# VectorE with one SBUF operand per instruction in the gather passes, and attention ends in seven groups

## What is computed

```python
x = _layernorm(x + _L0_gnn_ref(x, src, dst, ...))       # norm-weighted neighbour sum, 2 dense layers, gelu
x = _layernorm(x + _L1_gnn_ref(x, ..., src, dst, type)) # attention, 1 head, 8 relations
x = _layernorm(x + _L2_gnn_ref(x, src, dst, ...))       # neighbour sum, 2 dense layers, relu
x = _layernorm(x + _L3_gnn_ref(x, edge_attr, src, dst, ...)) # attention, 4 heads, edge scores
# an attention: logits of each edge, softmax over the edges of a destination, weighted sum
ex = jnp.exp(logits - seg_max[dst]); denom = segment_sum(ex, dst); out = segment_sum(ex / denom[dst] * z[src], dst)
```

## Time and profile before

| | |
|---|---|
| three timed runs, median (lowest, highest) | 10099.64 us (10096.38, 10099.9) |
| the profiled execution | 10036.1 us |
| its span | 10034.4 us |
| busy in the span: POOL, VectorE, ScalarE, TensorE | 7578.5, 3383.1, 1391.9, 493.3 us |
| the 16 DMA engines, mean share by the software queue and the hardware queue | 12.9%, 8.6% |

### The profile page before, as it was taken

The page is one execution under the profiler, slowest core; times in us unless marked ns, Lnnn a source line. Parts: engine busy times, 40 slices in busy tenths (PEclk is TensorE's granted clock), DMA queues, the critical chain, the costliest instruction groups (busy, mean ns, idle before and its releaser), DMA issues. The chain is left out here.

```text
span 10034.4 us, 21314 instructions
## 1 busy us (share of the span) xinstructions
PE 493.3 (5%) x3908; PEld 414.0 (4%) x3908; DVE 3383.1 (34%) x2929; ACT 1391.9 (14%) x1369; POOL 7578.5 (76%) x6764
## 2 busy tenths in 40 slices
PE   6000000000300000000000000000020000000000
PEld 6000000000200000000000000000020000000000
DVE  7222222222432222222225666666323222222222
ACT  0111111111211111111111111111111111111111
POOL 0777777777677777777767777777767777777776
PEclk9999999999655555555555555555555555555555
DMA  1211111111322121221222222222222212122221
GB/s 58 57 47 44 47 47 47 47 47 46 96 50 47 44 47 44 47 47 44 48 57 72 77 78 79 79 79 79 53 34 69 52 48 52 48 52 48 51 51 43
DMA packets 319095, 553.49 MB, mean 55 GB/s; under 512 B 157061, under 2 KB 164980, under 8 KB 311988
## 3 DMA queue, kind: packets, MB, share of 16 engines
q0 software_dynamic: 216064, 226.41, 12.9%
q1 hardware_dynamic: 102942, 326.10, 8.6%
HBM read 298.89 MB, written 253.15 MB: 55 GB/s over the span
## 5 line engine op out<-in xcount | busy, mean ns | idle before, releaser
L445 POOL DMA_INDIRECT rows_a<-table,idx_c_a x3224 | 3750.7, 1163 | 982.5 <-issue 982.5
L445 POOL DMA_INDIRECT rows_l<-table,idx_c_l x3224 | 3519.3, 1092 | 1229.3 <-issue 981.9
L862 DVE TENSOR_TENSOR score_a<-rows_a,target_a 128x26 f32<-128x26 f32 (+1 forms) x124 | 34.2, 276 | 3317.0 <-DMA rows_a<-table,idx_c_a 3317.0
L650 DVE COPY msg_l<-rows_l 128x1664 f32<-128x1664 f32 x124 | 197.2, 1591 | 2721.2 <-DMA rows_l<-table,idx_c_l 2721.2
L797 ACT COPY back_a<-msg_a 128x1690 f32<-128x1690 f32 (+1 forms) x124 | 416.7, 3361 | 516.0 <-DVE msg_a L902 516.0
L545 ACT COPY back_l<-msg_l 128x1664 f32<-128x1664 f32 x124 | 384.6, 3102 | 701.3 <-DVE msg_l L658 701.3
L787 ACT ACTIVATE diff_a<-diff_a 128x52 f32<-128x52 f32 (+1 forms) x124 | 38.6, 311 | 3171.0 <-DVE diff_a L879 3171.0
L436 ACT COPY idx_c_l<-src_i 128x26 int32<-128x26 int32 x124 | 25.8, 213 | 3263.0 <-DVE msg_l L650 3238.9
L902 DVE TENSOR_TENSOR_SCAN msg_a<-keeps_a,msg_a 128x1690 f32<-128x1690 f32 (+1 forms) x124 | 466.3, 3760 | 24.9 <-DVE msg_a L897 24.8
L658 DVE TENSOR_TENSOR_SCAN msg_l<-keeps_l,msg_l 128x1664 f32<-128x1664 bf16 x124 | 451.9, 3644 | 4.5
L419 DVE TENSOR_REDUCE part<-prod_e 125x132 f32<-125x8448 f32 x50 | 447.6, 8953 | 1.7
(11 more groups left out here) (228 smaller groups left out, 1721.3 us busy)
## 6 DMA issues: line engine op xcount, KB each, us to landing
prefix<-back_l SPq DMA_DIRECT2D x124, 832.0 KB, 3.6
prefix<-back_a SPq DMA_DIRECT2D x62, 936.0 KB, 3.7
prefix<-back_a SPq DMA_DIRECT2D x62, 858.0 KB, 3.5
rows_l<-table,idx_c_l POOLq DMA_INDIRECT x3224, 2.5
rows_a<-table,idx_c_a POOLq DMA_INDIRECT x3224, 2.5
feat<-edge_attr SPq DMA_DIRECT2D x50, 1031.2 KB
table<-stage SPq DMA_DIRECT2D x49, 260.0 KB, 2.1
spread<-zero SPq DMA_DIRECT2D x12, 806.0 KB
```

The lines of the kernel that those rows point to most:

```text
L445: pool.indirect_dma_start(rows[:, s * CH + k, 0:row], None, table, bass.IndirectOffsetOnAxis(idx_c[:, s, k:k + 1], 0))\
L650: nc.vector.tensor_copy(msg[:, u], rows[:, s * CH:(s + 1) * CH, :].rearrange("p k f -> p f k")).then_inc(taken, 1)
```

## The change

Inside the four passes every VectorE instruction has at most one operand that lies in SBUF; what it reads beside that lies in PSUM.

- `keeps` becomes one PSUM tile instead of two SBUF tiles. `msg` gets a column ahead of the 26 places; the last column of the chunk before is copied there by ScalarE (semaphore `carried`), and the scan runs over 27 columns. The steps L654, L894 and L897 are gone, and `same0` and `hold` with them.
- In `gather_sum` ScalarE instead of VectorE copies `rows` into `msg`; the order of ScalarE's work changes with it. The parts of the one-hots' comparison come from PSUM, per chunk, put there by ScalarE (`halve`), where two whole rows in bf16 were in SBUF.
- In `attend` scores, running maxima, differences and probabilities lie in two PSUM banks (`work_ps`, `prob_ps`). ScalarE copies the fetched scores in, and takes the exponential in two instructions. The curve of layer 3 takes two instructions where it took one. The running maximum gets a copy in SBUF (`best`).
- The end of an attention works in seven groups of seven blocks, each as soon as its rows land; the squares are VectorE's, the roots ScalarE's, and each group is stored by itself.

```diff
-                msg = tsb(f"msg_{tag}", [P, 2, D, CH])
-                keeps = tsb(f"keeps_{tag}", [P, 2, D, CH], BF16)
+                msg = tsb(f"msg_{tag}", [P, 2, D, 1 + CH])
+                keeps = tps(f"keeps_{tag}", [P, D, 1 + CH])
...
                         for c in range(CHUNKS):
-                            u = c % 2
+                            s, u = c % SLOTS, c % 2
+                            if c:
+                                act.wait_ge(scanned, c)
+                            nc.scalar.copy(keeps[:, :, 1:1 + CH], same16[:, c * CH:(c + 1) * CH].unsqueeze(1).broadcast_to([P, D, CH]))\
+                                .then_inc(keeps_ready, 1)
+                            if c:
+                                nc.scalar.copy(msg[:, u, :, 0:1], msg[:, 1 - u, :, CH:1 + CH]).then_inc(carried, 1)
+                                keep_back(c - 1)
+                            if first and c + HSLOTS < CHUNKS:
+                                act.wait_ge(hot_ready, 2 * (c + 1))
+                                halve(c + HSLOTS)
+                            act.wait_ge(gathered[s], 16 * CH * (c // SLOTS + 1))
+                            if c >= 2:
+                                act.wait_ge(back_ready, c - 1)
+                            nc.scalar.copy(msg[:, u, :, 1:1 + CH], rows[:, s * CH:(s + 1) * CH, :].rearrange("p k f -> p f k")).then_inc(taken, 1)
                             if c + SLOTS < CHUNKS:
                                 lists(act, idx_c, src_i, taken, chunk_ready, c + SLOTS)
...
                             if first and c + HSLOTS < CHUNKS:
                                 dve.wait_ge(counted, c + 1)
-                                one_hots(c + HSLOTS, hot_ready)
-                            dve.wait_ge(gathered[s], 16 * CH * (c // SLOTS + 1))
-                            if c >= 2:
-                                dve.wait_ge(back_ready, c - 1)
-                            nc.vector.tensor_copy(msg[:, u], rows[:, s * CH:(s + 1) * CH, :].rearrange("p k f -> p f k")).then_inc(taken, 1)
+                                hots(c + HSLOTS)
+                            dve.wait_ge(keeps_ready, c + 1)
...
-                            nc.vector.tensor_tensor_scan(flat, keeps[:, u].rearrange("p f k -> p (f k)"), flat, 0.0, ALU.mult, ALU.add)\
+                            nc.vector.tensor_tensor_scan(flat, keeps[:].rearrange("p f k -> p (f k)"), flat, 0.0, ALU.mult, ALU.add)\
                                 .then_inc(scanned, 1)
```

In `attend`, ScalarE's and VectorE's loops:

```diff
                         for c in range(CHUNKS):
...
+                            if c:
+                                keep_back(c - 1)
+                                nc.scalar.copy(msg[:, u, :, 0:1], msg[:, 1 - u, :, CH:1 + CH]).then_inc(carried, 1)
+                                act.wait_ge(diff_ready, c)
+                            act.wait_ge(gathered[s], 16 * CH * (c // SLOTS + 1))
+                            nc.scalar.copy(score, rows[:, s * CH:(s + 1) * CH, score_at:score_at + heads].rearrange("p k h -> p h k")).then_inc(score_in, 1)
                             act.wait_ge(diff_ready, c + 1)
-                            nc.scalar.activation(diff[:, u], diff[:, u], ACT.Exp).then_inc(exp_ready, 1)
+                            nc.scalar.activation(prob, diff[:, 0:heads], ACT.Exp).then_inc(exp_ready, 1)
+                            nc.scalar.activation(fall[:], diff[:, heads:2 * heads], ACT.Exp).then_inc(exp_ready, 1)
...
-                            dve.wait_ge(gathered[s], 16 * CH * (c // SLOTS + 1))
-                            link(nc.vector.tensor_tensor(score[:], fetched[:, :, score_at:score_at + heads].rearrange("p k h -> p h k"), target[:, :, here], ALU.add))
+                            dve.wait_ge(score_in, c + 1)
+                            link(nc.vector.tensor_tensor(score, score, target[:, :, here], ALU.add))
...
+                            for h in range(heads):
+                                last = nc.vector.tensor_tensor_scan(best_ps[:, h, 1:1 + CH], mneg16[:, here], score[:, h], best_ps[:, h, 0:1], ALU.add, ALU.max)
+                                chain.on(last)
...
+                            link(nc.vector.tensor_copy(best[:, u], best_ps))
+                            link(nc.vector.tensor_tensor(diff[:, heads:2 * heads], best[:, u, :, 0:CH], best_ps[:, :, 1:1 + CH], ALU.subtract))
...
-                                link(nc.vector.tensor_tensor(by_head(hold[:]), by_head(msg[:, 1 - u, :, CH - 1]),
-                                                             diff[:, u, heads:2 * heads, 0:1].broadcast_to([P, heads, part]), ALU.mult))
-                                dve.wait_ge(taken, c + 1)
-                                link(nc.vector.tensor_tensor(msg[:, u, :, 0], msg[:, u, :, 0], hold[:], ALU.add))
...
+                        centre(0)
+                        for g in range(1, NG):
+                            centre(g)
+                            finish(g - 1)
+                        finish(NG - 1)
```

257 lines of the change are left out of this document (131 added, 126 removed).

## The result

| | median us | runs | ratio to before |
|---|---|---|---|
| before | 10099.77 | 4 (10096.38 to 10103.22) | |
| changed | 9962.54 | 4 (9960.60 to 9966.73) | 0.9865 (95%: 0.9848 to 0.9882) |

The change gains 137 us where 1170 were forecast; 9962.54 lies 953 us above the range. The execution shown took 9966.73 us, its span 9965.0.

A forecast was written before the change was run, and what follows sets the result against it. POOL's gathers were taken to bound the kernel, held by VectorE reading two SBUF operands or the two-way copy. 10034.4 - 1155 + 4 - 17 + 3 = 8869 us of span, carried to 8930 us timed; range 8850 to 9010.

The forecast's parts named there:

- What bounds the kernel, and what holds a gather: All four passes: POOL's gathers bound; two SBUF reads by VectorE or the two-way copy hold them; 1155 us removable.
- Rival 1: Chunk scans: a scan holds gathers even with `keeps` in PSUM; 715 us of the 1155, 9645 us; chance 0.06.
- Rival 3: Gather passes: only the two-way copy is cured, 169 us and 10 us of ends; 9920 us; chance 0.02.
- Rival 4: All passes: a busy VectorE holds gathers wherever operands lie, only the ends gain; 10090 us; chance 0.01.
- The one-hots: Pass l0: reading PSUM costs VectorE about 134 us and the end nothing, as long as gathers bound.
- The ends: Ends of both attentions: 15.4 us after the last landing become 6.8; -17 us in all, between -10 and -22.
- The sum: Whole kernel: 10034.4 - 1155 + 4 - 17 + 3 = 8869 us of span.
- The step that failed: Span to timed median: the 63.5 us between profiled execution and timed runs was carried over, giving 8930 us.
- Nothing reaches POOL: Chunk loop: VectorE's added work, 8.7 us in l0 and 21.6 in l2, stays under POOL's 32.5 us per chunk.
- the means of 0.944 to 0.96 us a gather: All passes, profile after: gathers nearly bare, 6448 of them some 6115 us busy.
- My own last sentence: All gathers: forecast wrong if the bare gather exceeds 0.944 us with the faster stream, or run-end gathers 1.1 us.
- Rival 2: Chunk loop through PSUM becomes the bound, up to about 10980 us; sign: POOL waits for an index copy; chance 0.03.

The follow-up runs named there:

- fast group: Batches of runs in which the kernel before takes 10037 to 10052 us.
- e1_vector_waits: Changed kernel, but in all four passes VectorE waits for landed gathers and tells ScalarE by a tiny memset; 8853.74 us (0.8813).
- e2_hots_from_sbuf: Changed kernel, but operands of the l0 one-hots lie in SBUF as bf16 again, without ScalarE's copies per chunk; 8915.32 us (0.8875).
- e8_before_again: The kernel before, unedited, run and traced again beside the changed kernel; 10104.87 us.
- e9_vector_waits_2: The text of e1_vector_waits, unedited, run again beside the changed kernel and the kernel before; 9899.09 us.
- slow group: Batches of runs in which the kernel before takes 10076 to 10148 us.
- i2_keeps_in_sbuf_l: Changed kernel, but `keeps` lies in SBUF as bf16 again in gather passes l0 and l2; 9728.04 us.
- j1_keeps_in_sbuf_all: Changed kernel, but `keeps` lies in SBUF in all four passes, bf16 in gather passes, f32 in attentions; 9785.91 us (0.9666).

## Why the prediction was wrong

- **What bounds the kernel, and what holds a gather.** Right, as far as the fast group goes. Beside scans (3.98 us) and multiplies (3.34 us) gathers are bare in e1_vector_waits, and the passes together take 8073 us against 9234 of before in the fast group: 1161 us less, where 1155 were summed. The sentence of the Trainium skill that was weighed there ("SBUF — State Buffer", "Who interferes with whom", the inferred one) is not borne out here: the multiply of two SBUF tiles held a gather for 3.45 us, and with one operand in PSUM the gather beside it takes 0.94. Rivals 1, 3 and 4 fall by the bare gathers beside multiply and scan.
- **The one-hots.** Right that reading PSUM costs VectorE (3621 ns instead of 1878) and that POOL gains: with SBUF operands (e2_hots_from_sbuf) 62 gathers of l0 are held beside a one-hot and the pass takes 2082 us, with PSUM ones (e1_vector_waits, whose wait differs as well) it takes 2019.
- **The ends.** Right: in the changed kernel 6.4 us pass from the last landing to the last product, for 15.4 (forecast 6.8):

```profile
9954.77 0.19 DVE L973 TENSOR_SCALAR rows_a<-agg 128x28 f32<-128x28 f32 x1 [3.73 <-DMA agg<-prefix,endrow]
...
9960.59 0.62 DVE L991 TENSOR_TENSOR xcur<-rows_a 128x448 f32<-128x448 f32 x1
```

- **The sum.** 8869 us of span were forecast. In the fast group e1_vector_waits has 8852.2. The unedited changed kernel was never timed there. An estimate is the 8912.0 of e2_hots_from_sbuf less the 63 us that its l0 is longer than in e1_vector_waits, about 8849. So the sum was right, within some 20 us, for a condition in which the kernel was not timed.
- **The step that failed** is "The median of the timed runs lies 63.5 us above the profiled execution. Carried over as a fixed part it gives 8934, as a ratio 8927, not at all 8871." Half a per cent between a profile and its timed runs, where those agree among themselves within 7 us, was a sign that they were of two conditions (in the batch of e8_before_again, all of it slow, the profiled execution took 10107.93 us and the median of its runs is 10104.87), and the slow one has no fixed price. It costs the kernel before 72 us (10034.4 to 10106.2) and the text of e1_vector_waits 1055 (8852.2 to 9907.3 in e9_vector_waits_2): 915 in the passes, 140 around them. For the changed kernel itself the estimate is 9965.0 - 8849, some 1116. With it fell "Nothing reaches POOL" (16 waits in l0, 367 us) and the means of 0.944 to 0.96 us a gather (992 and 1052 ns). My own last sentence named this case ("if the bare gather itself came out longer than 0.944 with the faster stream"), and gave it no chance. Rival 2's sign, POOL waiting for an index copy, is there in l0, but PSUM traffic and the loop's own work do not bring it by themselves: nearly the same loop (e1_vector_waits) takes 2019 us in the fast group.
- **Where the gain went**, within the slow group (10106.2 to 9965.0, 141 us): a1 -130, l2 -7, a3 -154, l0 +118, l0 to a1 +32, l2 to a3 +8, the tail -8. The attentions had held gathers enough to lose down to 2226 us; l2 had not, and l0 lost. That the time falls at all was forecast for the right reason; that it falls by 137 us is what the slow group left of it.

**Open.** What makes a batch fast or slow, and what in the chip, or in the recording, sets 1.38 us a gather and multiples of 0.7 us on TensorE. Each timed run here carries its own span and granted clock, so it was recorded in some way as well. Semaphore events are missing above all where the pace is slow. A pass of the fast group has some 28,000 in its trace. The changed kernel has 4458, 4340, 3533 and 3770 in its four passes; i2_keeps_in_sbuf_l has 14,141 in l0 and 20,441 in l2, but 4414 and 3798 in a1 and a3; j1_keeps_in_sbuf_all has 16,840 in a1 and 4827 to 8382 in the others. The match is not strict: the kernel before in the slow group has 8281 in l0 and loses no time there. It fits a recording that can't keep up and stops the engines, but I only argue this; no run here was without a record.

## What to carry to other kernels

Before a profile's numbers are carried to timed runs, ask why the two differ: a gap nine times the spread of the runs (63.5 us to 7) came here from another condition, and a faster kernel may pay for it quite differently. When one of several edited versions is suddenly fast, run the unedited one beside it before believing the edit; here the same text took 8854 and 9899 us. On the change itself: one SBUF operand per VectorE instruction frees POOL's gathers (1161 us of four passes in the fast group), but in the slow group taking part of it back was worth more: the changed kernel with `keeps` of l0 and l2 in SBUF has the lowest time there (9728.04 us, 0.9625, 0.9608 to 0.9643), 235 us below the changed kernel of its batch. It was measured in one batch.

## What the runs showed that I had not expected

- The same kernel text in two groups of batches: 8853.74 and 9899.09 us; the kernel before 10048 and 10103 to 10135.
- In the slow group a1, l2 and a3 of the changed kernel take 2226 to 2235 us with 39 to 73 GB/s, 64 or 128 partitions, and with or without 1612 further DMAs. What they lose lies at the same places of each chunk.
- Matmuls of 0.24 us come 2.1, 2.8 or 3.5 us apart there, at a full granted clock, and also at half of it (1.2 GHz; 0.20 us, 2.80 apart in l2).
- With `keeps` in SBUF, which holds one gather per chunk for 3.87 us, a pass went from 2229 to 2193 us in one batch; in another the same text took 2214.
